# A Mamba-2 mixer on one Trainium2 core: decay masks for two groups of heads at once, and every engine's step order set anew

## The reference

```
h = layernorm(x) * (1 + ca) + sa
x = x + ga * attn(h)            # attn: Mamba-2 mixer, then an MLP, each with its residual
h = layernorm(x) * (1 + cb) + sb
x = x + gb * ffn(h)             # ffn: gated, 256 -> 1024 -> 1024 -> 1024 -> 256

mixer(xn):  z, xBC, dt = split(xn @ in_proj)
            dt = softplus(dt + dt_bias);  xBC = silu(causal_conv1d(xBC, 4 taps))
            per head (32 heads of 16, state 128):
               state_t = state_{t-1} * exp(dt_t * A) + dt_t * x_t (outer) B_t
               y_t     = state_t . C_t + D_skip * x_t
            y = rmsnorm(y * silu(z)) * rms_w;  return y @ out_proj
```

## Time and profile before

| | us |
|---|---|
| median of 3 runs | 3193.36 (3186.01 to 3193.88) |
| profiled execution, own time | 3180.88 |
| its span | 3179.2 |
| first and last mask of the mixer (L1121) | 138.8 to 1366.7 |
| TensorE busy over the span | 2799.2 (88%) |
| VectorE busy | 1839.9 (58%) |
| ScalarE busy | 1384.6 (44%) |
| GpSimd busy | 678.1 (21%) |

### The profile page before, as it was taken

How to read it: one execution, slowest core, us unless ns; L and a number is a source line. 1 busy time by engine, 2 the same in 40 slices (tenths; PEclk the granted TensorE clock), 3 DMA queues, 4 the chain that set the end, 5 groups by cost and what they waited for, 6 DMA issues and landing times. The chain is left out here.

```text
span 3179.2 us, 46142 instructions
## 1 busy us (share of the span) xinstructions
PE 2799.2 (88%) x16998; PEld 2086.3 (66%) x16998; DVE 1839.9 (58%) x3504; ACT 1384.6 (44%) x2394; POOL 678.1 (21%) x716
## 2 busy tenths in 40 slices
PE   0488888888888888869999799999999999999999
PEld 0354555455555555458888687887878787878787
DVE  4688888888888888746767433333333333333332
ACT  0566666666666666536555322222222222222221
POOL 5022222222222222210000122222222222222221
PEclk6799989998999899879999899999999999999999
DMA  3010101010101010035211100000000000000000
GB/s 125 29 35 20 35 20 35 20 35 20 35 21 35 21 35 11 28 104 208 70 62 64 48 13 7 11 14 16 14 16 14 16 14 16 14 16 14 16 14 8
DMA packets 104858, 107.06 MB, mean 34 GB/s; under 512 B 35897, under 2 KB 98617, under 8 KB 102977
## 3 DMA queue, kind: packets, MB, share of 16 engines
q1 hardware_dynamic: 99520, 103.81, 10.1%
q10 hardware_dynamic: 5120, 0.19, 0.1%
HBM read 71.41 MB, written 40.94 MB: 35 GB/s over the span
## 5 line engine op out<-in xcount | busy, mean ns | idle before, releaser
L1597 PE MATMUL fbank<-hid,fw 128*128 128x512 f32 x4096 | 962.3, 395 | 0.0
L1597 PEld LDWEIGHTS fbank<-hid,fw 128*128 128x128 f32 x4096 | 766.1, 187 | 187.0
L1747 DVE TENSOR_TENSOR hid<-fhf,hid 128x512 fp32r<-128x512 f32 x384 | 264.9, 690 | 704.3 <-POOL hid L1704 704.3
L1704 POOL TENSOR_SCALAR hid<-fhf 128x512 fp32r<-128x512 f32 x384 | 271.1, 706 | 1040.2 <-ACT fhf L1676 760.8
L808 ACT ACTIVATE mh<-ebank 128x512 f32<-128x512 f32 x512 | 302.0, 598 | 415.0 <-PE ebank L663 413.8
L1121 DVE SCALAR_TENSOR_TENSOR mh<-mh,gm 128x512 f32<-128x512 f32 x512 | 403.2, 794 | 1.8 <-ACT mh L808 1.8
L663 PE MATMUL ebank<-cright,cleft 102*128 102x512 bf16 x512 | 211.1, 413 | 64.1 <-ACT cin L847 28.9
L1676 ACT ACTIVATE fhf<-fbank,sh2c 128x512 f32<-128x512 f32 x128 | 88.0, 688 | 382.4 <-PE fbank L1597 382.4
L676 PE MATMUL yin<-mh,xpad 128*32 128x128 f32 x4096 | 230.5, 300 | 27.1 <-DVE mh L1121 26.6
L650 PE MATMUL ebank<-ah,win 128*128 128x512 f32 x640 | 246.7, 425 | 7.1 <-ACT cin L847 6.6
L1676 ACT ACTIVATE fhf<-fbank,sh1c 128x512 f32<-128x512 f32 x128 | 88.1, 688 | 320.8 <-PE fbank L1597 320.6
(11 more groups left out here) (180 smaller groups left out, 4380.1 us busy)
## 6 DMA issues: line engine op xcount, KB each, us to landing
fx<-x_d SPq DMA_DIRECT2D x17, 512.0 KB, 3.9
xs<-in_x SPq DMA_DIRECT2D x16, 512.0 KB, 4.3
h_d<-in_h SPq DMA_DIRECT2D x16, 512.0 KB, 5.4
o_d<-o SPq DMA_DIRECT2D x16, 512.0 KB, 2.9
mo<-o_d SPq DMA_DIRECT2D x16, 512.0 KB, 3.8
mx<-in_x SPq DMA_DIRECT2D x16, 512.0 KB, 4.8
x_d<-mx SPq DMA_DIRECT2D x16, 512.0 KB, 2.8
fw<-h_d SPq DMA_DIRECT2D x2, 4096.0 KB, 15.2
```

Of the source, the lines that this page charges most:

```text
L1597: mm = pe.matmul(bank[banks.slot(key)][:], w[:, k, m * P:(m + 1) * P].bitcast(dt), h[:, k, :].bitcast(dt), start=(k + n == 0), stop=(k == ...
L1704: pool.tensor_scalar(hid[i % 2][0][:, m, :], hf[j % 3][:], 1.0, 0.0, ALU.mult, ALU.add)\
L1747: dve.tensor_tensor(hid[i % 2][1][:, m, :], hf[j % 3][:], hid[i % 2][0][:, m, :].bitcast(F32), ALU.subtract).then_inc(c_lo.sem, 1)
```

## The change

Masks are made for two groups at once: `mh` becomes 4 tiles of two groups (8 slots in place of 7), `masked` runs in odd slots only, on 1024 columns, and `intra` runs six slots behind `decay`. ScalarE's `exponent` and TensorE's `intra` still work on one group; they count by pair.

Chunk steps get constants, as slots from the chunk's first slot, and `chunk_at` finds the chunk whose step stands in a slot:

| step | before | after |
|---|---|---|
| TensorE `project` | 16 | 17 |
| TensorE `state_decay`, `from_state` | 9 | 10 |
| TensorE `to_state` | 10 | 7 |
| TensorE `x_by_token`, `b_by_token` | -3, -2 | -3, -2 |
| ScalarE `y_out` | 16 | 15 |
| ScalarE `state_decay` | 10 | 10 |
| ScalarE `skip` | 11 | 6 |
| ScalarE `b_by_token` | -1 | -2 |
| GpSimd `gated`, `rms_power` | 10, 14 | 15, 20 |
| VectorE `new_state` | 8 | 8 |
| VectorE `addends` | 9 | 10 |
| VectorE `x_by_token`, `b_by_token` | -5, -4 | -6, -2 |
| VectorE `square_mean`, `residual` | 14, 15 | 15, 16 |

The constants of the block's steps change too (in the diff), the block gate from slot 26 to 25 among them. `new_state` waits in addition for its chunk's `from_state`. The bank orders follow the new slots, and ScalarE's, GpSimd's and TensorE's loops call the same functions at the new slots.

```diff
@@ -128,33 +128,50 @@
 STRIP = 32
 LEFT = 99 + P // STRIP - 1
 NEVER = -30000.0
-LAG = 5
-MH = 7
+LAG = 6
+MH = 8
 FIRST = -SPAN
-LAST = (CHUNKS + 1) * NG + 1
-
-NT_AT = (0, 1)
+LAST = (CHUNKS + 2) * NG + 1
+
+OP_AT = 17
+YOFF_AT = 10
+ST_AT = 7
+XT_AT = -3
+BT_AT = -2
+YSQ_AT = 15
+EC_AT = 10
+SKIP_AT = 6
+BCOPY_AT = -2
+GATED_AT = 15
+RMS_AT = 20
+STATE_AT = 8
+ADD_AT = 10
+XREAD_AT = -6
+GM_AT = -2
+MEAN_AT = 15
+RES_AT = 16
+NT_AT = (0, 2)
 AFFINE_AT = (1, 2)
 AL_AT = (0, 1)
-DT_AT = 3
-SOFTPLUS_AT = 4
-CHAIN_FROM = 1
+DT_AT = 5
+SOFTPLUS_AT = 5
+CHAIN_FROM = 2
 CHAIN_PER = 2
 CHAIN = SERIES + 13
-CONV_AT = (5, 7, 9, 11, 13, 15)
-EVAC_AT = (6, 8, 10, 12, 14, 16)
-TAPS_FROM = 4
-WEXP_AT = 15
-WV_AT = 12
+CONV_AT = (6, 7, 8, 12, 14, 15)
+EVAC_AT = (6, 7, 8, 12, 14, 16)
+TAPS_FROM = 5
+WEXP_AT = 16
+WV_AT = 14
 DTW_AT = 19
 DTW_READ_AT = 20
-Z_AT = (17, 19, 21, 23)
-Z_EVAC_AT = (18, 20, 22, 24)
-SILU_AT = 26
-TAIL_AT = 22
-LN_AT = (17, 20, 21, 22)
-LN_POW_AT = (18, 24)
-LN_NORM_AT = (23, 30)
+Z_AT = (18, 20, 22, 23)
+Z_EVAC_AT = (18, 20, 22, 23)
+SILU_AT = 25
+TAIL_AT = 30
+LN_AT = (14, 20, 22, 23)
+LN_POW_AT = (20, 30)
+LN_NORM_AT = (21, 28)
 
 
 def has_off(q):
...
+def chunk_at(S, at):
+
+    q, i = divmod(S - at, NG)
+    return q if i == 0 and has_chunk(q) else -1
 
 
 def act_bank_order():
...
-            yield ("bt", q + 1)
+        c = chunk_at(S, OP_AT)
+        if c >= 0:
+            yield ("op", c)
+        c = chunk_at(S, YOFF_AT)
+        if has_off(c):
+            yield ("yoff", c)
+        c = chunk_at(S, ST_AT)
+        if has_state(c):
+            yield ("st", c)
+        c = chunk_at(S, XT_AT)
+        if c >= 0:
+            yield ("xT", c)
+        c = chunk_at(S, BT_AT)
+        if c >= 0:
+            yield ("bt", c)
 
 
 FFN_SHAPES = ((KD, FF), (KD, FF), (KF, FF), (KF, FF), (KF, D))
...
     banks = Handover(sem, "bank", list(dve_bank_order()), 3)
     ebanks = Handover(sem, "ebank", list(act_bank_order()), 3)
     h_x = Handover(sem, "x", list(blocks), 1, fills=16, both=False)
     h_shsc = Handover(sem, "shsc", list(range(B)), 1, fills=16, both=False)
-    h_mh = Handover(sem, "mh", groups, MH)
+    h_mh = Handover(sem, "mh", [(q, i) for q in chunks for i in range(NG // 2)], MH // 2, uses=2)
     h_left = Handover(sem, "cleft", list(blocks), 2, fills=16 * 3 * NC, both=False)
     h_right = Handover(sem, "cright", list(chunks), 2, fills=48, both=False)
     c_yread = Count(sem, "yin_read", 0)
...
-    mh = [sb(f"mh{j}", [P, G4, P]) for j in range(MH)]
+    mh = [sb(f"mh{j}", [P, 2, G4, P]) for j in range(MH // 2)]
     ecs = [sb(f"ecs{j}", [P, QI, P]) for j in range(2)]
     yoff_s = sb("yoff_s", [P, QI, P])
     dx = sb("dx", [P, QI, P])
...
-                                   mh[h_mh.slot(key)][:, j, :], start=(i % 2 == 0), stop=(i % 2 == 1),
+                                   mh[h_mh.slot(key)][:, i % 2, j, :], start=(i % 2 == 0), stop=(i % 2 == 1),
                                    tile_position=(0, row))
                 mm.then_inc(h_mh.free(key), 1)
 
...
                 x_ = xc[q // NC % 2]
+                if q % NC == 0:
+                    pe.wait_ge(c_xc.sem, c_xc.at(0, q // NC + 1))
                 key = ("bt", q)
                 o = fresh(key)
                 pe.matmul(o[:, 0:P], x_[:, QI, tokens(q)], x_[:, QI + 1, tokens(q)], start=True, stop=True)\
...
                     decay(q, i)
                 if has_chunk((S - LAG) // NG):
                     intra(*divmod(S - LAG, NG))
-                if i == 0 and has_chunk(q - 2):
-                    project(q - 2)
-                if i == 1 and has_off(q - 1):
-                    state_decay(q - 1)
-                    from_state(q - 1)
-                if i == 2 and has_state(q - 1):
-                    to_state(q - 1)
-                if i == 5 and has_chunk(q + 1):
-                    x_by_token(q + 1)
-                if i == 6 and has_chunk(q + 1):
-                    b_by_token(q + 1)
+                c = chunk_at(S, OP_AT)
+                if c >= 0:
+                    project(c)
+                c = chunk_at(S, YOFF_AT)
+                if has_off(c):
+                    state_decay(c)
+                    from_state(c)
+                c = chunk_at(S, ST_AT)
+                if has_state(c):
+                    to_state(c)
+                c = chunk_at(S, XT_AT)
+                if c >= 0:
+                    x_by_token(c)
+                c = chunk_at(S, BT_AT)
+                if c >= 0:
+                    b_by_token(c)
                 if j < BLOCKS:
                     if n in NT_AT:
                         transposes(j, NT_AT.index(n))
...
             def exponent(q, i):
                 key = ("eb", q, i)
                 made(act, key)
-                act.wait_ge(h_mh.free((q, i)), h_mh.used_before(0, (q, i)))
-                nc.scalar.activation(mh[h_mh.slot((q, i))][:].rearrange("s h t -> s (h t)"), tile(key)[:],
+                pair = (q, i // 2)
+                act.wait_ge(h_mh.free(pair), h_mh.used_before(0, pair))
+                nc.scalar.activation(mh[h_mh.slot(pair)][:, i % 2].rearrange("s h t -> s (h t)"), tile(key)[:],
                                      ACT.Exp).then_inc(free(key), 1)
 
             def normalise(j, turn):
...
 
             def masked(q, i):
-                key = (q, i)
-                if i == 0:
+                key = (q, i // 2)
+                if i == 1:
                     released(dve, ("bt", q))
+                released(dve, ("eb", q, i - 1))
                 released(dve, ("eb", q, i))
-                m_ = mh[h_mh.slot(key)]
-                dve.scalar_tensor_tensor(out=m_[:], in0=m_[:], scalar=1.0,
-                                         in1=gm[q % 2][:].unsqueeze(1).to_broadcast([P, G4, P]),
+                m_ = mh[h_mh.slot(key)][:].rearrange("s g h t -> s (g h) t")
+                dve.scalar_tensor_tensor(out=m_, in0=m_, scalar=1.0,
+                                         in1=gm[q % 2][:].unsqueeze(1).to_broadcast([P, 2 * G4, P]),
                                          op0=ALU.min, op1=ALU.mult).then_inc(h_mh.full(key), 1)
 
             def addends(q):
-                last = (q, NG - 1)
+                last = (q, NG // 2 - 1)
                 dve.wait_ge(h_mh.free(last), h_mh.used(0, last))
                 if q:
...
+                    made(dve, ("yoff", q))
                     mark(dve.tensor_tensor(s3, s3, dec[q // NC % 2][:, q % NC, :].unsqueeze(2)
                                            .to_broadcast([P, NH, HD]), ALU.mult))
...
@@ -1171,20 +1214,26 @@
             for S in range(FIRST, LAST):
                 q, i = divmod(S, NG)
                 n, j = S % SPAN, S // SPAN + 1
-                if has_chunk(q):
+                if i % 2 and has_chunk(q):
                     masked(q, i)
-                if i == 0 and has_state(q - 1):
-                    new_state(q - 1)
-                if i == 1 and has_chunk(q - 1):
-                    addends(q - 1)
-                if i == 3 and has_chunk(q + 1):
-                    x_by_token(q + 1)
-                if i == 4 and has_chunk(q + 1):
-                    b_by_token(q + 1)
-                if i == 6 and has_chunk(q - 1):
-                    square_mean(q - 1)
-                if i == 7 and has_chunk(q - 1):
-                    residual(q - 1)
+                c = chunk_at(S, STATE_AT)
+                if has_state(c):
+                    new_state(c)
+                c = chunk_at(S, ADD_AT)
+                if c >= 0:
+                    addends(c)
+                c = chunk_at(S, XREAD_AT)
+                if c >= 0:
+                    x_by_token(c)
+                c = chunk_at(S, GM_AT)
+                if c >= 0:
+                    b_by_token(c)
+                c = chunk_at(S, MEAN_AT)
+                if c >= 0:
+                    square_mean(c)
+                c = chunk_at(S, RES_AT)
+                if c >= 0:
+                    residual(c)
                 if j < BLOCKS:
                     if n in AL_AT:
```

More of the change, by code:

```diff
@@ L180, in act_bank_order @@
             yield ("eb", q, i)
-        if i == 1 and has_off(q - 1):
-            yield ("ec", q - 1)
+        c = chunk_at(S, YOFF_AT)
+        if has_off(c):
+            yield ("ec", c)
         if j < BLOCKS:
@@ L308, in mixer @@
     blocks, chunks = range(BLOCKS), range(CHUNKS)
-    groups = [(q, i) for q in chunks for i in range(NG)]
     banks = Handover(sem, "bank", list(dve_bank_order()), 3)
@@ L914, in _ @@
                     exponent(q, i)
-                if i == 0 and has_chunk(q - 2):
-                    y_out(q - 2)
-                if i == 2 and has_off(q - 1):
-                    state_decay(q - 1)
-                if i == 3 and has_chunk(q - 1):
-                    skip(q - 1)
-                if i == 7 and has_chunk(q + 1):
-                    b_by_token(q + 1)
+                c = chunk_at(S, YSQ_AT)
+                if c >= 0:
+                    y_out(c)
```

(19 more changed lines are left out.)

20 lines of the change are left out of this document (5 added, 15 removed).

## The result

The changed kernel takes 3032.45 us (median of 4 runs, 3028.64 to 3034.99), against 3193.19 before: a ratio of 0.950, 95% interval 0.9482 to 0.9519. The profiled execution takes 3030.08 us, its span 3028.3.

What follows compares the result with a forecast made beforehand. VectorE was taken as the bound for some 55 us of a block, recovery from the gate for some 24. Gains of 2.6 + 0.7 + 0.5 = 3.8 us a block, x 15 = 57, gave 3193.4 - 57 = 3136 us, range 3105 to 3160.

Steps and rivals of the forecast that it cites:

- What bounds the kernel: Mixer block of 77.6 us: some 55 us of work for VectorE and some 24 us of recovery from the gate.
- The masks: VectorE's 512 narrow passes become 256 wide ones: 0.07 us saved a pair, 1.1 us a block, 18 us in all.
- The lag: `intra` six slots behind instead of five: slack unchanged for even slots, one more for odd; no cost counted.
- The banks: Banks freed at other slots, earlier by projection copies: helps TensorE only where VectorE is the bound; nothing counted outside the recovery.
- The recovery: Stretch from the block gate to the state update: earlier gate and shorter waits gain 2.6 us a block, the large term.
- T: Forecast time at which the block gate ends, 669.7 on the old trace's time axis.
- The clock: TensorE behind the gate: half clock at first, taken as full from T + 9, before the projection.
- The rms wait: VectorE's 14.4 us of waits for GpSimd's rms power go; 0.5 us a block counted; below 5 us in all expected.
- the half-clock one: TensorE's slots 28 to 34 behind the gate: clock stays low through the projection, 1.0 us a block lost, 3208; chance 0.17.
- the one blocked by GpSimd: VectorE's wide masks held by both GpSimd passes, 1.6 us more in each of 60 chunks, 3232; chance 0.05.
- The lead is kept: TensorE enters the gate further ahead or its clock doesn't fall: two thirds of 10.4 us go, 3073; chance 0.13.
- the 1.4 named as a sign of being wrong: VectorE's wide masks: above 1.4 us on average would show the forecast wrong; 1.21 us was expected.

Runs made afterwards that it cites:

- two_passes: The changed kernel with each pair's mask made as two passes of 512 columns back to back instead of one wide pass; 3067 us, ratio 0.962 to the kernel before.
- after_conv_old: The changed kernel with the projections and their copies at the old slots, copies a slot behind; 3169 us, ratio 0.991 to the kernel before.
- pairs_addends_10: The kernel before with pair masks, lag 6 and the old order, but VectorE's addends at slot 10 instead of 9; 3208 us, ratio 1.006.

## Why the prediction was wrong, point by point

**What bounds the kernel** held: VectorE over most of a block, the recovery from the gate in the rest.

**The masks** held in VectorE's time: 1.21 us each, and 1.1 us a block more work in `two_passes`. Their worth did not: 18 us were counted, and undoing the wide pass costs 34, since a wait came back with the work. A further 1.5 us of work a block (65.9 to 64.4) went with the new order even with narrow passes. The masks' time beyond their median fell with the change from (371.2 - 473 x 0.684) / 15 = 3.2 to (321.6 - 235 x 1.218) / 15 = 2.4 us a block (473 and 235 masks between the gates, with their busy time and median). Stretched masks, as the one at 657.59, lose that much less. That GpSimd's passes are what stretches them was not tested. The Trainium skill ("VectorE: DVE Perf Modes", the section on the TRN2 errata) would have put the wide pass at 40 us, by the prediction's estimate, and `two_passes` is 34 us slower. But its VectorE works only 16 us longer, as start-to-start times say, and the rest are waits, so the rule came near for another reason.

**The lag** failed: "The slack is unchanged" looked at the mask alone. `intra` of a chunk's last group is a slot later, and the old order with pairs lost 76 us, 59 of them by `addends` alone. The change had moved that step, so the error cost the sum nothing, but it hid why the step moved.

**The banks** failed, and this is the step that made the sum wrong: "Both help TensorE only where VectorE is the bound, so I count nothing outside the recovery". The term was put at nothing, and taking the copies back a slot costs 75 us, with the projections at their old places too 137. With late copies TensorE's projections wait 53.8 us for banks and VectorE's waits rise from 4.2 to 9.6 us a block. The step reads a lead as worthless where VectorE doesn't wait, but the lead that TensorE and ScalarE build there is still theirs when the gate comes: VectorE's stock is six groups in the change and four with late copies. That the cost goes by way of the stock is argued from this, not shown; other kernels of the table break the pattern, and in `after_conv_old` a third of VectorE's added waits is the one for `wexp`.

**The recovery** failed with it. It took the end of the exp of slot 25 from the old trace, 662.5, and VectorE at slot 21 then. In the new order that exp no longer stands behind a projection, so the gate starts with VectorE at slot 20, and 10.9 us lie between the gate's start and `addends` (665.36 to 676.28) where the prediction had 8.0 (662.5 to 670.5). The arithmetic behind it was near: the decay of slot 28 was forecast for T + 0.6 and came at T + 0.65 (673.78 against 673.13). But the wait of 2.2 us before `addends` did not come. The wait for the projection was 0.76 us in this block, not 4.3: it began at 681.62, with `ysq` at hand, T + 8.5 instead of T + 10.9, and ran at full clock.

**The clock** was forecast to return at T + 9, that is by 682. In this gate it was back by 678, T + 5:

```profile
674.00:677.00 3.00, 3.00 (x23) 1.36 (x22) 2.97 (x6) 2.90 (x7) 1.18 (x2) 0.50 0.00 0
678.00:688.00 10.00, 9.10 (x93) 5.91 (x92) 8.05 (x11) 7.54 (x16) 3.65 (x3) 1.00 0.25 83
```

It was low 5.5 us a block on average, against 13.5. The projection behind the gate (681.62) ran at full clock, in 1.99 us.

**The rms wait** fell from 14.4 to 4.6 us, as said. **The rivals**: the half-clock one didn't come. Nor did the one blocked by GpSimd with its 1.6 us more a chunk, though wide masks were stretched beside GpSimd's product (661.59); their mean of 1.37 us is just below the 1.4 named as a sign of being wrong. "The lead is kept" (3073, chance 0.13) came nearest, and even it was too small, since it counted two thirds of 10.4 us of waits and 1.1 of work; 7.4 and 2.6 went.

What stays open: the parts overlap (the wide pass, the copies, project, gate, state and skip taken back one at a time cost 34, 75, 54, 44, 41 and 15 us, 263 together, for a gain of 161), so no single share can be given; what besides the stock decides at a gate; what the low clock costs by itself; and why `pairs_addends_10` still is slower than the kernel before.

## What to carry to other kernels

Where one engine must be blocked for a fixed time (here 7 us of ScalarE for a table switch and two large silus), count how much finished input the bounding engine has in stock at that moment, and which work of the others can lie inside the block; a wait that is removed far ahead of it can pay there. The stock is a sign and not the whole: kernels with the same stock of four lie between 3087 and 3215 us here. Don't judge moves of a hand-written order one by one on the old order: three of them that are worth 54, 44 and 15 us in the new one cost 30 in the old. When the lag of one pipelined step grows, every reader of its last result moves with it.

## What the runs showed of the hardware that was not expected

The low TensorE clock can't be priced by filling TensorE's idle time alone. Matmuls that do nothing, put where TensorE waits for the gate, removed 9.9 us of low clock a block and gave a net 0.7 us a block, but the filler also moved TensorE's transposes from 1.3 us ahead of the gate's end to 1.8 us or more behind it. In the new order, where the filler delayed next to nothing, 3.0 us less of low clock gave nothing.
